# A two-layer transformer kernel: padding rows kept in DRAM, fills moved to POOL, fewer and other transfers at the entry of attention

## The reference, cut to what matters

```python
x = x + attn(_layernorm(x, axis=-1), WQ, WK, WV, WO)

def attn(x, WQ, WK, WV, WO):                 # S = 512, NUM_HEADS = 16, D_K = 8
    Q, K, V = (heads(WQ), heads(WK), heads(WV))
    score = einsum('bhqd,bhkd->bhqk', Q, K) / sqrt(D_K) + mask
    score = exp(score - max(score, axis=-1, keepdims=True))
    score = score / sum(score, axis=-1, keepdims=True)
    return einsum('bhqk,bhkd->bhqd', score, V)... @ WO
```

## Time and profile before

| what | value |
|---|---|
| median of 3 runs | 689.01 us (688.6 to 689.12) |
| span of the profiled execution | 687.3 us |
| around that span, median less span | 1.7 us |
| busy: PE, DVE, ACT, POOL | 574.4, 419.9, 301.6, 166.1 us |
| bytes moved | 38.82 MB, mean 56 GB/s |

### The profile page before, as it was taken

The page is one execution under the profiler, slowest core; times in us unless marked ns, Lnnn a source line. Parts: engine busy times, 40 slices in busy tenths (PEclk is TensorE's granted clock), DMA queues, the critical chain, the costliest instruction groups (busy, mean ns, idle before and its releaser), DMA issues.

```text
span 687.3 us, 9139 instructions
## 1 busy us (share of the span) xinstructions
PE 574.4 (84%) x3296; PEld 427.9 (62%) x3296; DVE 419.9 (61%) x1020; ACT 301.6 (44%) x431; POOL 166.1 (24%) x180
## 2 busy tenths in 40 slices
PE   2489999999999552999952868999999999998997
PEld 1445556565665331778841546768787888787866
DVE  6677778878878351143223898696559936763240
ACT  3235555455455420443421543563446534752351
POOL 3002112153172442000015843341410032001100
PEclk9799999999999855999995999999999999999999
DMA  3314222141220035483311110010000000000000
GB/s 104 125 59 169 86 102 86 36 151 66 62 66 12 20 111 175 137 253 96 107 42 28 34 28 1 1 31 1 1 16 0 1 1 0 16 1 0 17 1 15
DMA packets 40909, 38.82 MB, mean 56 GB/s; under 512 B 3104, under 2 KB 31776, under 8 KB 40864
## 3 DMA queue, kind: packets, MB, share of 16 engines
q1 hardware_dynamic: 38816, 34.04, 15.6%
q0 software_dynamic: 2048, 4.20, 2.1%
HBM read 23.54 MB, written 14.68 MB: 56 GB/s over the span
## 4 chain that ended last, share of the span: by engine, by line
PE 61%; DVE 15%; issue 8%; ACT 6%; POOL 5%; DMA 2%; SPq 1%; DVEq 0%; POOLq 0%; ACTq 0%
PE ps L1820 6%; PE ps L1782 6%; PE ps L1773 5%; PE ps L1842 5%; PE ps L1527 4%; PE ps L1923 4%; PE ps L1556 4%; PE ps L1919 4%; PE ps L1920 4%; PE ps L1843 4%; PE ps L1846 3%; DVE pm L961 3%; PE ps L1544 3%; POOL xs_dram L497 2%; PE ps L1836 2%
## 5 line engine op out<-in xcount | busy, mean ns | idle before, releaser
L642 ACT ACTIVATE PT<-ps 128x768 f32<-128x768 f32 (+1 forms) x96 | 84.6, 882 | 81.3 <-PE ps L1544 79.8
L961 DVE TENSOR_REDUCE pm<-ps 128x4 f32<-128x512 f32 x160 | 104.3, 685 | 22.8 <-PE ps L1530 13.3
L511 POOL TENSOR_SCALAR_AFFINE_SELECT PT<-PT 128x512 f32<-128x512 f32 x64 | 39.8, 634 | 152.3 <-ACT PT L642 152.3
L1527 PE MATMUL ps<-KP,QS 128*128 128x512 f32 x160 | 66.8, 448 | 5.6 <-DVE pm L961 3.8
L1544 PE MATMUL ps<-QM,KP 128*128 128x512 f32 (+3 forms) x256 | 61.5, 343 | 0.7 <-DVE QM L975 0.7
L1556 PE MATMUL ps<-PT,V 128*32 128x128 f32 (+3 forms) x512 | 45.9, 453 | 12.1 <-POOL PT L511 12.1
L722 ACT ACTIVATE HT<-ps,cols 128x640 f32<-128x640 f32 x32 | 25.4, 794 | 57.8 <-PE ps L1773 57.8
L1527 PEld LDWEIGHTS ps<-KP,QS 128*128 128x128 f32 x160 | 29.0, 191 | 33.7 <-DVE pm L961 31.4
L1544 PEld LDWEIGHTS ps<-QM,KP 128*128 128x128 f32 x256 | 39.8, 192 | 10.2 <-issue 4.5
L1331 DVE TENSOR_TENSOR_SCAN zero<-decay,OG 128x512 f32<-128x512 f32 x32 | 42.3, 1322 | 1.1
L1782 PE MATMUL ps<-W,HT 128*128 128x128 f32 x320 | 37.9, 278 | 3.3 <-ACT HT L722 3.3
(11 more groups left out here) (278 smaller groups left out, 1287.7 us busy)
## 6 DMA issues: line engine op xcount, KB each, us to landing
qk_dram<-HL SPq DMA_DIRECT2D x8, 512.0 KB
W<-in_eW SPq DMA_DIRECT2D x16, 256.0 KB, 3.4
QS<-qk_dram SPq DMA_DIRECT2D x64, 48.0 KB
KP<-qk_dram SPq DMA_DIRECT2D x64, 48.0 KB
xs_dram<-zero SPq DMA_DIRECT2D x4, 640.0 KB, 5.2
XS<-xs_dram SPq DMA_DIRECT2D x8, 320.0 KB, 4.4
ys_dram<-zero SPq DMA_DIRECT2D x8, 320.0 KB, 2.9
qk_dram<-HL SPq DMA_DIRECT2D x8, 256.0 KB
```

The costliest lines, as they stand in the source:

```text
L511: g.affine_select(out=diag, in_=diag, pattern=[[0, 4], [1, P]], compare_op=ALU.is_ge, fill=0.0, base=0, channel_multiplier=-1).then_inc(se ...
L642: act.activation(PT[:, 2 * i:2 * i + 2, a:z], ps[:, 2 * (n % 2) + 2:2 * (n % 2) + 4, 0:z - a], ACT.Exp, scale=float(DK) ** -0.5).then_inc( ...
L961: v.tensor_reduce(pm[:, t, k, :], bank[n % 2].rearrange("p (i n) -> p i n", n=P), AXX, ALU.max).then_inc(pair_free[n % 2], 1)
L1527: mm = pe.matmul(to, QS[:, G % 2, t * P:(t + 1) * P], KP[:, G % 3, k, :, :].rearrange("p i n -> p (i n)"), start=True, stop=t != k)
```

## The change

- `qk_dram` holds 32 rows a head in place of 24: rows 24 to 31 are padding, zeros for queries and 1.0 for keys, written from two constant tiles (`store_pads`), two transfers of 256 KB a batch.
- A group's queries come in one transfer of 128 rows in place of four of 24; its keys in four transfers of 32 rows in place of four of 24. So there are five transfers in place of eight.
- The planes are stored in six transfers of 256 KB, each as soon as its half is written, in place of two of 512 KB and two of 256 KB behind the split.
- The fills of QS and the 1.0 fills of KP go; KP's zero fills move from DVE to POOL, between and behind the two first roots. POOL's other fills are put in another order.
- `const` and `cols` are issued from ACT's queue. On SP's queue WQ and WK follow quarter 0, the other weights follow x, and three row constants go behind the pads of groups 0 and 1. PE waits for the weights where each is used.

```diff
-        qk_dram = nc.dram_tensor("qk_dram", [NB, 2, 3 * P, SEQ], F32, kind="Internal").ap()
+        qk_dram = nc.dram_tensor("qk_dram", [NB, 2, H, 32, SEQ], F32, kind="Internal").ap()
+        ones = low["h2_w"][:, FF - 1, :].bitcast(F32)
...
-                    sp.dma_start(const[:, :], d["const"]).then_inc(par_in, 16)
-                    sp.dma_start(cols[:, :], d["cols"]).then_inc(par_in, 16)
-                    for t, n in ((wq, "WQ"), (wk, "WK"), (wv, "WV"), (wo, "WO"), (wr, "Wr")):
-                        sp.dma_start(t[:, :], d[n]).then_inc(w0_in, 16)
-            for i, n in enumerate(("bo", "b2", "w3_s")):
-                sp.dma_start(rows[:, i, :], d[n].partition_broadcast(P)).then_inc(w1_in, 16)
+                    for t, n in ((wq, "WQ"), (wk, "WK")):
+                        sp.dma_start(t[:, :], d[n]).then_inc(wqk_in, 16)
+            for t, n in ((wv, "WV"), (wo, "WO"), (wr, "Wr")):
+                sp.dma_start(t[:, :], d[n]).then_inc(w0_in, 16)
...
+            def store_pads(b):
+
+                sp.wait_ge(zero_set, 1)
+                sp.dma_start(qk_dram[b, 0, :, 24:32, :], zero[:, 0:SEQ]).then_inc(pads_out[b], 16)
+                sp.wait_ge(ones_set, 1)
+                sp.dma_start(qk_dram[b, 1, :, 24:32, :], ones).then_inc(pads_out[b], 16)
+
             def store_planes(b):
 
+                sp.wait_ge(parts, 2 * b + 1)
+                for c in (0, 2):
+                    sp.dma_start(qk_dram[b, 0, :, 8 * c:8 * c + 8, :], HL[:, 0, 0, :].bitcast(F32)).then_inc(q_planes, 16)
                 sp.wait_ge(halves, 2 * b + 1)
-                q, k = qk_dram[b, 0], qk_dram[b, 1]
-                sp.dma_start(q[0:2 * P, :].rearrange("(c p) n -> p c n", p=P), HL[:, 0, :, :].bitcast(F32)).then_inc(planes, 16)
-                sp.dma_start(q[2 * P:3 * P, :], HL[:, 0, 0, :].bitcast(F32)).then_inc(planes, 16)
+                sp.dma_start(qk_dram[b, 0, :, 8:16, :], HL[:, 0, 1, :].bitcast(F32)).then_inc(q_planes, 16)
+                sp.wait_ge(parts, 2 * b + 2)
+                for c in (0, 1):
+                    sp.dma_start(qk_dram[b, 1, :, 8 * c:8 * c + 8, :], HL[:, 1, 0, :].bitcast(F32)).then_inc(k_planes, 16)
                 sp.wait_ge(halves, 2 * b + 2)
-                sp.dma_start(k[P:3 * P, :].rearrange("(c p) n -> p c n", p=P), HL[:, 1, :, :].bitcast(F32)).then_inc(planes, 16)
-                sp.dma_start(k[0:P, :], HL[:, 1, 0, :].bitcast(F32)).then_inc(planes, 16)
+                sp.dma_start(qk_dram[b, 1, :, 16:24, :], HL[:, 1, 1, :].bitcast(F32)).then_inc(k_planes, 16)
 
             def pad(G):
 
                 b, g = G // NG, G % NG
-                q = qk_dram[b, 0].rearrange("(c h k) n -> h c k n", c=3, k=DK)
-                k = qk_dram[b, 1].rearrange("(c h k) n -> h c k n", c=3, k=DK)
                 if g == 0:
-                    sp.wait_ge(planes, 64 * (b + 1))
-                if G < 2:
-                    sp.wait_ge(qs_set, 1)
-                else:
+                    sp.wait_ge(pads_out[b], 32)
+                    sp.wait_ge(q_planes, 48 * (b + 1))
+                if G >= 2:
                     sp.wait_ge(tp_free, TURNS["max", G - 2] + 1)
-                for i in range(4):
-                    sp.dma_start(QS[32 * i:32 * i + 24, G % 2, :].bitcast(F32), q[4 * g + i]).then_inc(qs_in[G % 2], 16)
+                sp.dma_start(QS[:, G % 2, :].bitcast(F32),
+                             qk_dram[b, 0, 4 * g:4 * g + 4].rearrange("h r n -> (h r) n")).then_inc(qs_in[G % 2], 16)
+                if g == 0:
+                    sp.wait_ge(k_planes, 48 * (b + 1))
                 if G < 3:
-                    sp.wait_ge(kp_set, 5 * G + 5)
+                    sp.wait_ge(kp_set, G + 1)
                 else:
                     sp.wait_ge(ts_full, NKU * (G - 2))
                 for i in range(4):
-                    sp.dma_start(KP[32 * i:32 * i + 24, G % 3, :, i, :].bitcast(F32), k[4 * g + i]).then_inc(kp_in[G % 3], 16)
+                    sp.dma_start(KP[32 * i:32 * i + 32, G % 3, :, i, :].bitcast(F32), qk_dram[b, 1, 4 * g + i]).then_inc(kp_in[G % 3], 16)
+            store_pads(0)
             store_planes(0)
             pad(0)
             pad(1)
+            for b in range(1, NB):
+                store_pads(b)
+            for i, n in enumerate(("bo", "b2", "w3_s")):
+                sp.dma_start(rows[:, i, :], d[n].partition_broadcast(P)).then_inc(w1_in, 16)
...
         @block.gpsimd
         def _(g):
-            g.memset(zero[:, :], 0.0).then_inc(setup, 1)
-            g.memset(mhalf[:, :], -0.5).then_inc(setup, 1)
+            def set_keys(s):
+                g.memset(KP[:, s, :, :, :].bitcast(F32), 0.0).then_inc(kp_set, 1)
+
+            g.memset(mhalf[:, :], -0.5).then_inc(mhalf_set, 1)
+            g.memset(zero[:, :], 0.0).then_inc(zero_set, 1)
+            g.memset(ones, 1.0).then_inc(ones_set, 1)
...
+            first_rsqrt(0, slice(0, TB))
+            set_keys(0)
+            first_rsqrt(1, slice(TB, NT))
+            set_keys(1)
             g.memset(V[:, :, :], 0.0).then_inc(setup, 1)
-
+            g.wait_ge(setup, 1)
+            g.memset(V[:, :, DK:DK + 1], 1.0).then_inc(setup, 1)
+            set_keys(2)
...
         @block.scalar
         def _(act):
+            act.dma_start(const[:, :], d["const"]).then_inc(par_in, 16)
+            act.dma_start(cols[:, :], d["cols"]).then_inc(par_in, 16)
             act.wait_ge(par_in, 32)
...
-            v.memset(QS[:, :, :].bitcast(F32), 0.0).then_inc(qs_set, 1)
-
-            def set_keys(s):
-                v.memset(KP[:, s, :, :, :].bitcast(F32), 0.0).then_inc(kp_set, 1)
-                v.wait_ge(kp_set, 5 * s + 1)
-                for i in range(4):
-                    v.memset(KP[32 * i:32 * i + 32, s, :, i, :].bitcast(F32), 1.0).then_inc(kp_set, 1)
-
-            set_keys(0)
...
             make_halves(0)
-            set_keys(1)
             first_norm(1)
             first_norm(2)
-            set_keys(2)
             first_norm(3)
...
             pe.wait_ge(par_in, 32)
-            pe.wait_ge(w0_in, 80)
...
             first_turn(0)
             pe.wait_ge(tc0, 1)
+            pe.wait_ge(wqk_in, 32)
             project(0)
             first_turn(1)
+            pe.wait_ge(w0_in, 48)
             first_v(0)
```

More of the change, by code:

```diff
@@ L271, in build @@
         ys_dram = nc.dram_tensor("ys_dram", [DUMP, P], F32, kind="Internal").ap()
-        qk_dram = nc.dram_tensor("qk_dram", [NB, 2, 3 * P, SEQ], F32, kind="Internal").ap()
+        qk_dram = nc.dram_tensor("qk_dram", [NB, 2, H, 32, SEQ], F32, kind="Internal").ap()
         x_in = [sem(f"x_in{b}") for b in range(NB)]
         par_in = sem("par_in")
+        wqk_in = sem("wqk_in")
         w0_in = sem("w0_in")
@@ L287, in build @@
         parts, halves = sem("parts"), sem("halves")
-        planes = sem("planes")
-        qs_set, kp_set = sem("qs_set"), sem("kp_set")
+        q_planes, k_planes = sem("q_planes"), sem("k_planes")
+        pads_out = [sem(f"pads_out{b}") for b in range(NB)]
+        zero_set, mhalf_set, ones_set, kp_set = sem("zero_set"), sem("mhalf_set"), sem("ones_set"), sem("kp_set")
         qs_in = [sem(f"qs_in{s}") for s in range(2)]
@@ L349, in _ @@
                 if b == 0:
-                    sp.dma_start(const[:, :], d["const"]).then_inc(par_in, 16)
-                    sp.dma_start(cols[:, :], d["cols"]).then_inc(par_in, 16)
-                    for t, n in ((wq, "WQ"), (wk, "WK"), (wv, "WV"), (wo, "WO"), (wr, "Wr")):
-                        sp.dma_start(t[:, :], d[n]).then_inc(w0_in, 16)
-            for i, n in enumerate(("bo", "b2", "w3_s")):
-                sp.dma_start(rows[:, i, :], d[n].partition_broadcast(P)).then_inc(w1_in, 16)
+                    for t, n in ((wq, "WQ"), (wk, "WK")):
+                        sp.dma_start(t[:, :], d[n]).then_inc(wqk_in, 16)
+            for t, n in ((wv, "WV"), (wo, "WO"), (wr, "Wr")):
+                sp.dma_start(t[:, :], d[n]).then_inc(w0_in, 16)
             zv = xs_dram[0:DUMP, :].rearrange("(p r) n -> p (r n)", p=P)
             def clear_slots(i):
-                sp.wait_ge(setup, 1)
+                sp.wait_ge(zero_set, 1)
                 sp.dma_start(zv[:, i * 10 * P:(i + 1) * 10 * P], zero[:, :]).then_inc(zeroed, 16)
@@ L464, in _ @@
         def _(g):
-            g.memset(zero[:, :], 0.0).then_inc(setup, 1)
-            g.memset(mhalf[:, :], -0.5).then_inc(setup, 1)
[L467 to L472, removed]
+            def set_keys(s):
[3 more added lines that the diff above has]
+            g.memset(ones, 1.0).then_inc(ones_set, 1)
+            g.wait_ge(mhalf_set, 1)
             def first_rsqrt(i, c):
@@ L478, in _ @@
             first_rsqrt(0, slice(0, TB))
+            set_keys(0)
             first_rsqrt(1, slice(TB, NT))
+            set_keys(1)
+            g.memset(V[:, :, :], 0.0).then_inc(setup, 1)
+            g.wait_ge(setup, 1)
             g.memset(V[:, :, DK:DK + 1], 1.0).then_inc(setup, 1)
-            g.wait_ge(setup, 6)
+            set_keys(2)
```

(11 more changed lines are left out.)

## The result

The changed kernel takes 685.12 us (median of 5 runs, 683.93 to 685.65) against 689.07 before in the same comparison: ratio 0.9929, interval 0.9904 to 0.9953. It is faster by 4.0 us, where 9.9 was forecast; the range, 676.3 to 683.0, does not hold it. The profiled span is 683.8 us.

The account below looks back on a forecast made before the run. The wait for the first scores at 33.76 us, behind VectorE's fills and the transfers, was taken as the bound at the entry. 9.6 + 0.3 = 9.9 off the 687.3 span gives 677.4, plus 1.7 is 679.1 us; range 676.3 to 683.

Parts of the forecast that it names:

- Part 2: KP and V fills on POOL at the entry: cost nothing, 0 taken for POOL and VectorE holding each other up.
- Norms that wait while POOL fills: Entry: a named sign that the prediction is wrong, as POOL's fills were taken to cost VectorE 0.
- that case: Entry: POOL's fills block VectorE's norms through the shared port; first score 25.5 to 27, time 680.5 to 682.5; chance 0.20.
- Part 1: Start of VectorE: statistics begin at 3.8, not 7.20 (bounds 3.6 and 5.4); rows to the k split move up 3.4.
- Part 3: TensorE at the entry: batch 1's norm ends at 15.8, then three turns and four projections, mostly fast; done at 22 to 23.
- Part 4: Stores and key reads at the entry: planes landed at 19.4, group 0's last keys at 24.1 (22.9 to 27).
- The lower end of my range: First score of group 0 at 21.9, with both entry legs at their best.
- Part 5: After the entry: 9.6 saved at first scores, 0.3 more at group 3's key wait; extra traffic costs nothing.
- everything behind moves up whole: All stages after the first score: tied by waits, they keep the full 9.6 saved there.
- Stores on few engines: Plane stores run at 62 to 70 GB/s, scores start at about 39; 694 to 727 us; chance 0.07.
- the two legs: Entry: the transfer leg lies about 2 us below TensorE's, so shortening either alone gives little.
- Cold or slow leg: Entry: clock falls after the k projection, or slow issues and reads; first score 26.7 or 27, 681.7 to 682; chance 0.15.

Follow-up runs that it names:

- fills behind norms: The changed kernel with POOL's KP slot 0 fill held until the first norm ended, its other fills until the last; ratio to before 0.9897.
- idle time: The changed kernel with slot 0 filled by VectorE while waiting for X, slots 1 and 2 by POOL before the first root, V after the norms; ratio 0.9888.
- fills alone: The kernel before, with old transfers and loads, only the fills moved to where no norm runs; ratio to before 0.9943.
- on ACT: The changed kernel with KP's slots filled by ACT beside the norms, not by POOL, and V filled by POOL behind the last norm; ratio to before 0.9873.
- joined: The changed kernel with fills in the engines' idle time and const and cols behind X's first quarter on SP's queue; ratio to before 0.9874.
- Transfers alone: The kernel before with only the new pad rows, plane stores and group reads, VectorE keeping all its fills; ratio to before 0.9996.
- kept busy: The kernel with idle-time fills and const behind X, plus 12 and 8 products of zeros on TensorE before its first two turns; ratio to before 0.9865.

## Why the prediction was wrong, step by step

**The step that failed** is Part 2: "I take 0" for VectorE and POOL holding each other up. I took the bound below from the fill of V beside VectorE's fills, which is a row on another operation of VectorE; no row before showed a POOL fill beside a norm. The runs put 2.37 - 1.12 = 1.25 us on both legs and 4.93 - 1.12 = 3.81 on TensorE's leg, and took both away by moving the fills to another time or to another engine. Norms that wait while POOL fills were the first sign of being wrong that the prediction named. The rule of the Trainium skill (SBUF — State Buffer, "Who interferes with whom"), an exclusive lock between the two engines which a tensor-scalar operation can take, fits these runs: norm held up by POOL and not by ACT (1.12), statistics and the subtraction from PSUM not held up (2.35 and 0.69 us). I gave that case 0.20 and priced it at 680.5 to 682.5, too low: I let norms 1 to 3 end along with the fills and left one turn and two projections behind them, 2.7 us. In the run norm 1 alone took all three fills, and three turns and four projections, 7.1 us, were still to come.

**Part 1.** Mis-sized: X landed after 4.0 us and not the 3.0 behind my 3.8; the start was 4.91. const beside X caused it: with const behind X, 2.9. The bound (5.4) held it, the value taken did not.

**Part 3.** The size held, the reason did not. From norm 1 to the first score I had 6.2 to 7.2 us, and 7.1 were measured. But I expected TensorE fast because its gap would be only 2.6 us. Five kernels have that gap (2.68 us) and short norms, and their turns and projections took 7.7 (fills behind norms), 6.5 (idle time), 6.5 (fills alone), 6.8 (on ACT) and 6.9 us (joined). In the first three TensorE was still slow from the start, until 22.59, 19.78 and 19.54; in the last two the granted clock fell to 0.50 at 18.84 and 17.32, under the work that followed the gap. I had taken the engine for fast when the gap began, and had no row that said so. In the changed kernel the sum is this: 15.8 (my end of norm 1) + 1.1 (X) + 1.25 + 3.81 = 22.0, measured 22.2; 7.1 more gives the measured first score, 29.3.

**Part 4.** Right in kind: the pads' reads spread over the engines and the leg ends near 25 where nothing delays its start. Its terms erred in opposite directions: 0.60 to 0.63 an issue and not 0.75, but 7.3 us from first store to last landing and not 7.0 (the last store took 4.2 to land, not 3.3), at 277 to 307 GB/s in the timed stretches. In the joined kernel the leg ended at 24.66; 24.1 was forecast. In the changed kernel it was not the bound. The lower end of my range, a first score at 21.9 with both legs best, does not follow from my own legs: the transfer leg's best was 22.9, and the later leg counts.

**Part 5.** Right: group 3's wait is gone (TensorE's waits up to 266 us hold none for KP), and the lead, 3.7 us at group 2's QM addition (66.30 and 62.58), is 4.3 at that of group 3 (78.03 and 73.77). The extra traffic cost nothing visible there. But "everything behind moves up whole" was too good by 0.9 in these two executions: 4.42 us were won at the first score, 3.97 at the end of the maxima, 3.5 in the span. The first 0.45 is the clock: it fell to 0.50 at 36.9, and the four turns of the maxima took 1.09 us and not 0.63. By group 3 the lead was back at 4.3; the rest, 4.2 at 212 us, 3.9 at the first expert product and 3.5 at the end, is of the size by which the same code differs between executions (the 419.8 against 415.9 above), and its cause stays open.

**The rivals.** Stores on few engines: did not happen, DMA share 0.97. Transfers alone: nothing, as the reading of the two legs said. Cold or slow leg: its clock condition came true in part (0.50 from 19.9 to 26.7), in a gap that the held-up norm had made 6.5 us long. The combined forecast, 9.9 us, is nearly reached without the collision of fills and norms: ratios 0.9865 to 0.9874 (on ACT, joined, kept busy) are 8.7 to 9.3 us of 689, while 0.9888 and 0.9897 (idle time, behind norms) are 7.7 and 7.1.

## What to carry to other kernels

When work is moved from a busy engine to an idle one, list which operations will run at the same moment, and look for a row of that very pair; a row of another operation on the same two engines is no evidence. Fills are best put where both engines idle anyway, ahead of the first input; cutting them into pieces helped one norm here and not the other. When two legs end within a few microseconds of each other, price each half of a change alone and both together: here the transfers were worth 0 alone and about 5 us at the first score with the fills, and a second load that starts beside the first input may take from the very transfer that the chain begins with.

## What the runs showed of the hardware

A POOL fill of 1.80 us and VectorE's tensor-scalar operation exclude each other for whole instructions (four in 4.93 us in place of 1.11; with the fills in quarters 1.44 in one place, 2.48 in another; a 128x4 one 0.83 in place of 0.17), while the same fill by ACT (1.90 us) costs it nothing. Two loads issued at the same moment on two queues slow each other: 256 KB in 4.0 us and 220 KB in 3.4, against 2.9 and 2.7 with the second half a microsecond behind on the first one's queue. By its durations TensorE begins at the lower of its two levels, and a window's 1.00 says nothing before the trace's first clock record: a 128x512 product took 2.07 us ahead of that record and 1.13 behind it. And the clock's place is a matter of small shifts: the first scores came at 25.63 with fills on ACT and at 24.66 in the joined kernel, but from 28 to 34 us the row scores ran at 1.00 in the one and at 0.50 in the other (next to last but one number of the windows below), so that the maxima were done 9.0 us behind the first score in the one and 10.7 in the other.

```profile
28.00:34.00 6.00, 3.60 (x10) 1.51 (x10) 5.29 (x11) 0.00 (x0) 0.00 (x0) 1.00 0.88 273
```

```profile
28.00:34.00 6.00, 4.43 (x8) 1.67 (x7) 4.64 (x9) 0.00 (x0) 0.00 (x0) 0.50 0.83 258
```
